# Matmuls of constants with unread results on TensorE, in the gaps of an attention chain and around a router

## The reference, cut to what matters

```python
x = x + attn(layernorm(x))
x = x + ffn(layernorm(x))
# attn: q = h@Wq+bq, k = h@Wk+bk, 16 heads of 16
#   q_w = softmax((q@Wqa+bqa)*s, over tokens);  pooled_q = sum of q_w*q
#   qk = k*pooled_q;  k_w = softmax((qk@Wka+bka)*s, over tokens); pooled_k = sum of k_w*qk
#   out = (pooled_k*q)@Wt + bt + q
# ffn: n = rmsnorm(h)*norm_weight
#   out = shared MLP(n) + sum over the top 2 of 8 experts, weights from sigmoid(n@router_w.T)
#   each MLP: relu(n@w1+b1)@w2+b2, 256 -> 1024 -> 256
```

## Time and profile before

| what | value |
|---|---|
| median of three runs | 828.69 us (827.51 to 830.9) |
| the profiled execution's own time | 826.31 us |
| its span, first to last instruction | 824.5 us |
| mean granted TensorE clock | 0.969 |
| busy: TensorE, VectorE, ScalarE, GpSimd | 91%, 69%, 54%, 22% |

### The profile page before, as it was taken

One profiled execution on the slowest core, in us unless ns is written; L12 is line 12 of the kernel. 1 busy time (PEld: TensorE's weight loads), 2 busy tenths in 40 slices (PEclk: granted clock), 3 DMA queues, 4 the chain that ended last, 5 costly groups with the idle time before them and its releaser, 6 DMA issues. The chain is left out here.

```text
span 824.5 us, 11746 instructions
## 1 busy us (share of the span) xinstructions
PE 752.6 (91%) x4254; PEld 620.0 (75%) x4254; DVE 570.5 (69%) x1179; ACT 442.8 (54%) x739; POOL 185.0 (22%) x163
## 2 busy tenths in 40 slices
PE   3588998888998999989989989989999989998987
PEld 3345665567886889879878979878888979897776
DVE  6633666589576568666775767666766767677995
ACT  3541134535533764665847485755857485747332
POOL 2200111000000404332523334442433332220000
PEclk9878999799999999999999999999999999999999
DMA  9200012100050234462634564452744564333860
GB/s 331 109 1 2 26 64 74 42 1 0 1 211 1 64 115 160 145 236 84 240 143 145 169 235 149 155 196 102 255 151 144 183 224 151 116 135 107 279 200 32
DMA packets 45657, 106.80 MB, mean 130 GB/s; under 512 B 9277, under 2 KB 33600, under 8 KB 37920
## 3 DMA queue, kind: packets, MB, share of 16 engines
q1 hardware_dynamic: 38784, 88.36, 30.9%
q0 software_dynamic: 6816, 17.71, 6.5%
HBM read 89.26 MB, written 17.69 MB: 130 GB/s over the span
## 5 line engine op out<-in xcount | busy, mean ns | idle before, releaser
L712 PE MATMUL psD<-w,hhi 128*128 128x512 f32 x824 | 301.1, 406 | 16.2 <-DVE x_sb L1160 11.9
L867 ACT ACTIVATE hid<-psU,b 128x512 f32<-128x512 f32 (+2 forms) x280 | 153.5, 576 | 248.9 <-issue 172.9
L713 PE MATMUL psD<-w,hlo 128*128 128x256 f32 x824 | 233.0, 283 | 0.0
L692 PE MATMUL psU<-xhl,w 128*128 128x512 f32 (+2 forms) x560 | 194.9, 348 | 15.7 <-DVE w L1166 13.9
L1137 DVE TENSOR_TENSOR hlo<-hid,hhi 128x512 fp32r<-128x512 f32 x206 | 141.1, 691 | 91.8 <-ACT hhi L870 89.3
L712 PEld LDWEIGHTS psD<-w,hhi 128*128 128x128 f32 x824 | 156.4, 190 | 58.6 <-DVE x_sb L1160 13.8
L693 PE MATMUL psU<-xhl,w 128*128 128x512 f32 (+2 forms) x560 | 194.8, 348 | 0.0
L694 PE MATMUL psU<-xhl,w 128*128 128x512 f32 (+2 forms) x560 | 194.3, 347 | 0.0
L713 PEld LDWEIGHTS psD<-w,hlo 128*128 128x128 f32 x824 | 156.3, 190 | 0.2
L397 POOL DMA_INDIRECT xin<-token_in,src x71 | 79.1, 1115 | 297.2 <-PE psT L668 154.2
L692 PEld LDWEIGHTS psU<-xhl,w 128*128 128x128 f32 x560 | 106.9, 191 | 32.4 <-DVE w L1166 16.1
(11 more groups left out here) (196 smaller groups left out, 607.3 us busy)
## 6 DMA issues: line engine op xcount, KB each, us to landing
raw<-in_wpack SPq DMA_DIRECT2D x30, 1024.0 KB, 7.8
xT<-in_wpack SPq DMA_DIRECT2D x28, 1024.0 KB, 7.2
xT<-token_out SPq DMA_DIRECT2D x32, 256.0 KB, 4.4
x_sb<-in_x SPq DMA_DIRECT2D x8, 512.0 KB, 9.3
token_in<-z_sb SPq DMA_DIRECT2D x8, 512.0 KB, 2.9
out<-x_sb SPq DMA_DIRECT2D x16, 256.0 KB, 4.7
b<-in_b2pack SPq DMA_DIRECT2D x29, 128.0 KB, 3.6
att<-in_attn SPq DMA_DIRECT2D x1, 1379.0 KB, 11.5
```

The lines of the kernel that those rows point to most:

```text
L692: mm(acc, whi[:, slot, col], xhl[:, k, 0, 0:rows], start=(k == 0), stop=False)
L712: mm(acc, hhi[:, part], w[:, slot, :, col], start=(c == 0), stop=False)
L713: last = mm(acc[:, 1, :], hlo[:, part], whi[:, slot, col], start=False, stop=(c == MH - 1))
L867: last = nc.scalar.activation(hid[:, n % 4, i * rows:(i + 1) * rows], acc, ACT.Relu, bias=b1[:, u % 2, m:m + 1])
```

## The change

A helper `busy(bank, n)` issues n matmuls of the unit matrix with 256 columns of constants into the left half of a bank. No instruction reads the result; whatever uses the bank next overwrites it. There are 24 such matmuls in twelve places of TensorE's list: ten places in the attention chain (17 matmuls), one ahead of router(1) (four) and one behind it (three). Two waits are added where a bank must be free: xnT_ready for the full 16 (`NT // 2`), and x1_ready for the full 16. No other engine's list changes.

```diff
--- before.py
+++ after.py
@@ -591,6 +591,11 @@
 
 
 
+            def busy(bank, n):
+
+                for _ in range(n):
+                    mm(bank[:, 0:256], ident, cst[:, 0:256], start=True, stop=True)
+
             pe.wait_ge(cst_loaded, 16)
             for q in range(4):
                 turn_rows(q)
@@ -603,25 +608,34 @@
             turn_rows(10)
             turn_rows(11)
             turn_max(0)
+            busy(psU[:, 3, :], 2)
             turn_rows(12)
             turn_rows(13)
             spread_max(0)
+            busy(psU[:, 3, :], 3)
             turn_probs(0)
             turn_rows(14)
             turn_rows(15)
             pool_rows(0)
             score(1)
+            busy(psU[:, 3, :], 1)
             turn_pooled(0)
+            busy(psU[:, 3, :], 1)
             project_pooled(0)
             turn_max(1)
+            busy(psU[:, 3, :], 2)
             fold_key(0)
             spread_max(1)
             score(2)
             turn_probs(1)
+            pe.wait_ge(xnT_ready, NT // 2)
+            busy(psT[:, 0, :], 1)
             turn_max(2)
             pool_rows(1)
             spread_max(2)
+            busy(psT[:, 0, :], 1)
             turn_pooled(1)
+            busy(psT[:, 0, :], 1)
             turn_probs(2)
             project_pooled(1)
             pool_rows(2)
@@ -630,8 +644,10 @@
             score(3)
             project_pooled(2)
             turn_max(3)
+            busy(psT[:, 0, :], 3)
             mix(0)
             spread_max(3)
+            busy(psT[:, 0, :], 2)
 
             project_chunk(0)
             turn_probs(3)
@@ -650,7 +666,10 @@
                 if c == NC // 2 + 2:
                     router(0)
                 turn_chunk(c - 2)
+            pe.wait_ge(x1_ready, NT // 2)
+            busy(psU[:, 3, :], 4)
             router(1)
+            busy(psU[:, 3, :], 3)
 
             def ranks():
```

## The result

Four executions of the changed kernel gave a median of 820.22 us (817.61 to 822.96) beside 829.4 us (827.51 to 830.9, four executions) for the kernel before: a ratio of 0.9891 with a 95% interval of 0.985 to 0.9932. The forecast was 824.1 us in a range of 820.5 to 829.5, so the median lies 0.3 us under the range, and the gain is twice the one forecast. The two intervals overlap; I take the gain as 7 to 9 us. That is about 1%, a small gain, and both intervals lie clear of 1. The profiled pair differs by 7.1 us: 819.21 against 826.31 us, spans of 817.4 and 824.5.

The account below looks back on a forecast made before the run. TensorE, busy 91%, was taken as the bound, with about 20 us of its attention chain at half clock. Terms -7.2 + 0.2 + 1.6 + 0.8 + 0 gave -4.6 us: median 824.1 us, range 820.5 to 829.5.

Parts of the forecast that it names:

- the surviving stretch: Attention chain: one of four half-clock stretches in effect survives and takes away 1.6 us of the gain (bounds 0 and 5).
- the router: Around router(1): four fillers ahead start at half clock and delay it, +0.8 us; three behind are covered, 0 us.
- the first term: Transposes and probabilities from 36.7 to 43.6 us: full clock gains 1.4 us, with ScalarE's row copies pacing both transpose groups.
- The other terms: Later chain at full clock: fold_key(0) and score(2) gain 2.6 us, pool_rows(2) 1.5 us, mix(0) 1.7 us.
- the singles' overhangs: Single fillers in the chain's short gaps stick out 0.0 to 0.1 us each; 0.2 us charged for all, between 0 and 0.6.
- the sum's better side: Best case at router(1): unbroken work brings the clock back at once, router(1) falls to 1.92 us, -0.7 us in all.
- Everything holds: No half clock before 77 us and the router's fillers bring the clock back: some -7.3 us, 821.4 us; chance 0.18.
- Transposes don't hold the clock: The stretch 36.7 to 43.6 us stays at half clock, its gain is lost and fillers overhang: 826.7 us; chance 0.11.
- Off the path: ScalarE's and VectorE's small steps and new clock falls take most of the gain; 1 us left, 827.7 us; chance 0.11.
- The slower rival: Matmuls of constants, mostly zeros, don't hold the clock, so fillers only cost place: +5.2 us, 833.9 us; chance 0.10.

Follow-up runs that it names:

- narrow: Only the attention chain's 17 fillers, each replaced by two 16-column matmuls, against the kernel before: 826.54 us, ratio 1.0002.
- router_only: Only the seven fillers around router(1), the chain's 17 left out, against the kernel before: 826.87 us, ratio 0.9986.
- after: The changed kernel with all 24 fillers, first measurement and profile, against the kernel before: 820.22 us, ratio 0.9891.
- after2: The changed kernel measured and profiled again without edit, six executions, against the kernel before: 821.99 us, ratio 0.9915.
- chain_only: The changed kernel without the seven fillers and their wait around router(1); ratio to the kernel before 0.9895, 819.35 us.
- router_before: The changed kernel without the three fillers behind router(1); ratio to the kernel before 0.9891, 818.54 us.
- late_gap: Chain's fillers, with five before turn_chunk(6), three before turn_chunk(7), two before router(1), none after; against the kernel before: 816.3 us, ratio 0.9876.
- slot_gaps: Chain's fillers plus three after the down product of each of seven 128-row expert slots; against the kernel before: 815.08 us, ratio 0.9856.
- both_gaps: Fillers of late_gap and slot_gaps joined, against the kernel before: 812.38 us, ratio 0.9803.
- early_too: both_gaps plus four fillers before turn_rows(6) and two before score(0); ratio to the kernel before 0.9789, 810.78 us.
- turns: Only the chain's fillers, each replaced by three transposes of 128 columns, against the kernel before: 820.91 us, ratio 0.9913.

## Why the prediction was wrong

**The mechanism was right.** The chain's time at half clock was the price, the fillers take it away, and an earlier first projection reaches the end undiminished. narrow shows that it is the clock and not the time filled. The expert part took 669 us in both profiles. The steps that failed are terms of the sum, mis-sized: the surviving stretch first of all, then the router and the first term.

**The sizes were not.** Taken from the profiled pair and the parts:

- *First term, "I take 0.4 + 0.46 + 0.55 = 1.4 us".* Measured 2.05 us. Against the start of score(0), turn_probs(0) came 0.6 us sooner (I had 0.4), it took 0.46 less, as costed, and the second group of transposes took 1.04 us and not 1.92, the whole 0.88. I had let ScalarE's row copies pace both groups. They pace the first: in the changed kernel ScalarE goes from its copies to the first exponentials without a pause. Behind the second group stands pool_rows(0), which TensorE reaches in its own order.
- *The other terms.* score(1) to score(2) 0.7 us less (fold_key 0.9), score(2) to score(3) 3.3 us where score(2) held too (1.7 + 1.5), mix(0) and what follows 1.6 (1.7). These hold in the pair, and so do the singles' overhangs. How often the kernel before has the falls at pool_rows(2) and mix(0) is open: they are in its two profiles, and not in those of router_only and narrow.
- *"I let one of the four stretches in effect survive and take away 1.6 us".* It did so in the first profile, at score(2), the place named. But of seven profiles with the chain's fillers as in the change, and no others ahead of them (after, after2, chain_only, router_before, late_gap, slot_gaps, both_gaps), one has a fall there, and the other six have none in the chain. By these the charge should have been about 1.6 / 7, some 0.2 us, an estimate from few profiles (in early_too, with fillers ahead of the chain too, two stretches survive). Over the executions this is the largest of the errors. I had taken it from how narrow the matmuls around the fillers are, with no row for it.
- *The router, "I take +0.8 us".* Measured -0.3 in the pair, -0.3 to +0.5 over the profiles. The clock came back before the router began, as the sum's better side had it.

In the profiled pair the charge was in fact paid, and the miss is made up in another way: 7.1 us measured less 4.6 forecast is 2.5 us, of which 1.1 are the router, 0.65 the first term, 0.55 the earlier start that no filler made, and 0.2 the singles' overhangs and the rest. The remaining 1.4 us of the 3.9 by which the median missed are that the profiled execution lay 2.4 us under the median before, and only 1.0 after.

With 2.05 for 1.4, 0.2 for 1.6 and 0.1 for 0.8 the sum is -7.4 us, or 821.3 us from the same median. The two measurements of the changed kernel lie on both sides of it (820.22 and 821.99 us). That the first fell 0.3 us outside the range is partly chance, for the second lies inside; that the gain was put at half its size is not.

**The rivals.** "Everything holds", with its chance of 0.18 and 821.4 us, was the case of six of the seven profiles in the chain and stood at too low a chance; the argument for it, that the largest gap left is smaller than one that had passed without a fall, was the better one, and in after2 even a gap of 1.51 us (before the transposes at 36.35 us) passed without a fall. "Transposes don't hold the clock" falls with turns, by its ratio and by the rise at 41.9 us. "Off the path" falls with the 669 us and with the first projection, 6.7 us sooner. The slower rival, that matmuls of constants don't hold the clock, falls with every profile that has them in the chain.

**The range** was too narrow below: it held the full gain only for an execution like the profiled one of before, and the difference of two medians of a few executions, each with its own falls, moves by 1 to 2 us.

## What to carry to other kernels

Read the granted clock beside the timeline of a chain of short dependent steps: a TensorE busy for most of it can still run at half clock, and each us there went with 0.44 us of this kernel's span. Wide matmuls or transposes with unread results, as many as the gap holds at full clock, took most of that away here; 16-column ones didn't, and twice as many wide ones gave half of it back. Put them in the gap ahead of the fall, not behind it: seven around the router returned nothing, ten that begin at the gap ahead of the last but one turns made the way from the last turns to the first expert product 2.3 us shorter. And look at the clock of several executions before taking one profile's falls for the kernel's.

## What was not expected of the hardware

In narrow the clock fell at 51.3 us although the gaps ahead of fold_key(0) were filled with 16-column matmuls and TensorE had been busy for 6.27 of the 6.5 us up to 51.4; the busy share did not tell here whether the clock would fall. In turns it rose at 41.9 us after transposes alone. A single filler takes 0.6 to 0.7 us from its first record's start to its last one's end (44.70 us in the first profile after), but the next one behind it starts about 0.43 us later, less than the 0.47 us taken from mix. The lengths of the stretches at half clock made the same program's span differ by 8 us.
